# Turning x-hat of a cross-attention block with VectorE blocks and four SBUF transfers instead of TensorE transposes

## What is computed

```python
tgt1 = _layer_norm(tgt, g1, be1)
tgt = tgt + _self_attn(tgt1, mask, Wq, bq, Wk, bk, Wv, bv, Wo, bo)
tgt = tgt + (memory @ Wg.T + bg)
tgt1 = _layer_norm(tgt, g2, be2)
ff = jax.nn.relu(tgt1 @ W1.T + b1) @ W2.T + b2
return tgt + ff
```

## Time and profile before

| | |
|---|---|
| median of 3 runs | 1756.23 us (1755.37 to 1756.37) |
| profiled execution | 1755.81 us, span 1754.0 us |
| PE busy | 1724.6 us, 98% |
| ACT busy | 1432.4 us, 82% |
| DVE busy | 1359.8 us, 78% |
| POOL busy | 802.2 us, 46% |
| DMA | 200.46 MB, mean 114 GB/s |
| granted PE clock | 0.8 to 0.9 of full speed in the first two of 40 slices, then 0.9 or more |

### The profile page before, as it was taken

The page is one execution under the profiler, slowest core; times in us unless marked ns, Lnnn a source line. Parts: engine busy times, 40 slices in busy tenths (PEclk is TensorE's granted clock), DMA queues, the critical chain, the costliest instruction groups (busy, mean ns, idle before and its releaser), DMA issues. The chain is left out here.

```text
span 1754.0 us, 53678 instructions
## 1 busy us (share of the span) xinstructions
PE 1724.6 (98%) x17780; PEld 1698.0 (97%) x17780; DVE 1359.8 (78%) x6945; ACT 1432.4 (82%) x5567; POOL 802.2 (46%) x782
## 2 busy tenths in 40 slices
PE   6799999999999999999999999999999999999998
PEld 6799999999999999999999999999999999999998
DVE  7777777787787777787787877877777877877874
ACT  4788888888888888888888888888888888888883
POOL 4244444444444454444444444444444444444444
PEclk8899999999999999999999999999999999999999
DMA  5333333333333332333433333333333333333320
GB/s 173 106 127 107 115 123 107 120 121 107 122 119 106 124 120 95 132 115 99 135 111 104 129 111 110 128 109 113 124 106 120 121 107 122 118 109 122 119 83 31
DMA packets 185796, 200.46 MB, mean 114 GB/s; under 512 B 18864, under 2 KB 135984, under 8 KB 185520
## 3 DMA queue, kind: packets, MB, share of 16 engines
q1 hardware_dynamic: 185520, 197.02, 33.9%
HBM read 62.73 MB, written 16.78 MB: 45 GB/s over the span
## 5 line engine op out<-in xcount | busy, mean ns | idle before, releaser
L404 ACT ACTIVATE scores<-scores,row_min 128x128 f32<-128x128 f32 x2048 | 795.3, 402 | 11.5 <-DVE row_min L651 11.5
L780 POOL TENSOR_TENSOR hT_lo<-hid,hT_hi 128x512 fp32r<-128x512 f32 x256 | 354.6, 1385 | 516.3 <-DVE hT_hi L685 516.3
L651 DVE CUSTOM_DVE_ANT_0 scores<-score_ps,mask_bias 128x128 f32<-128x128 f32 x2048 | 472.2, 286 | 0.9 <-issue 0.6
L416 ACT ACTIVATE probs<-turn_ps 128x512 f32<-128x512 f32 x512 | 304.8, 596 | 163.7 <-PE turn_ps L916 163.5
L404 ACT ACTIVATION_READ_ACCUMULATOR scores<-scores,row_min 128x1 f32 x2048 | 411.8, 201 | 0.0
L916 PE MATMUL turn_ps<-ident,scores 128*128 128x128 f32 x2048 | 307.6, 273 | 3.1 <-ACT probs L416 3.1
L850 PE MATMUL ffn_ps<-w_hi,hT_lo 128*128 128x256 f32 x1024 | 300.6, 294 | 0.5 <-ACT hid L446 0.5
L850 PE MATMUL ffn_ps<-zT_hi,w_lo 128*128 128x256 f32 x992 | 292.1, 294 | 0.3 <-ACT hid L446 0.3
L852 PE MATMUL ffn_ps<-w_hi,hT_hi 128*128 128x256 f32 x1024 | 284.8, 278 | 0.0
L851 PE MATMUL ffn_ps<-w_lo,hT_hi 128*128 128x256 f32 x1024 | 284.5, 278 | 0.0
L851 PE MATMUL ffn_ps<-zT_lo,w_hi 128*128 128x256 f32 x992 | 276.1, 278 | 0.0
(11 more groups left out here) (136 smaller groups left out, 4268.4 us busy)
## 6 DMA issues: line engine op xcount, KB each, us to landing
q_stack<-q_hi SPq DMA_DIRECT2D x128, 256.0 KB, 2.4
k_stack<-k_hi SPq DMA_DIRECT2D x256, 128.0 KB, 2.3
x_in<-x_dram SPq DMA_DIRECT2D x64, 256.0 KB, 2.6
mem_in<-memory_dram SPq DMA_DIRECT2D x64, 256.0 KB, 3.0
x_res<-x_dram SPq DMA_DIRECT2D x64, 256.0 KB, 3.0
q_stack<-q_lo SPq DMA_DIRECT2D x64, 256.0 KB, 2.4
k_stack<-k_lo SPq DMA_DIRECT2D x128, 128.0 KB, 2.3
inv<-inv_cols SPq DMA_DIRECT2D x256, 64.0 KB, 2.2
```

Source lines behind the costliest of these rows:

```text
L404: last = act.activation(exps, exps, ACT.Exp, bias=row_min[:, k, h:h + 1], scale=-1.0, accum_out=row_sum[:, k, h:h + 1])
L416: act.activation(probs[:, k, :], turn_ps[k % 2][:, :], ACT.Copy).then_inc(probs_copied[k % 2], 1)
L651: last = dve.tensor_tensor_reduce(out=scores[:, slot(i, t), h, :], in0=score_ps[t % 2][:, h * S:(h + 1) * S], in1=mask_bias[:, b, :], scal ...
L780: pool.tensor_tensor(halves[1], src, halves[0], ALU.subtract).then_inc(done, 1)
```

## The change

x-hat of groups 1 to 63 is no longer turned by PE. DVE writes it in place over `x_in`, then turns it in blocks of 32 by 32 with two transposes into `x_quads` (`turn_quads`); four transfers of 64 KB within SBUF carry the blocks back into `x_in` so that each partition holds its feature. POOL makes both parts of `xT` from there, the high part as a product with one; group 1 is split by DVE. Group 0 goes by PE as before. The first norm moves forward in the iteration: statistics at t 3, `rstd` at t 4, apply at t 5, blocks at t 8. The load of x moves to the start of SP's iteration and waits for the split; the store of y moves behind the spread of the inverses. The turn of z stays where it is.

```diff
+        def quad_rows(w):
+            return w[:].rearrange("p b (k c j) -> p b k j c", j=QUADS, c=32)
+        def quad_blocks(w):
+            return w.rearrange("p (j k b r) -> p b k j r", j=QUADS, k=KT, b=GB)
+        def quad_cols(w):
+            return w[:].rearrange("p b n -> p (b n)").rearrange("p (i m r) -> p m i r", i=QUADS, r=32)
+        def in_order(w):
+            return w[:].rearrange("p k (b i r) -> p (k b) i r", b=GB, i=QUADS)
...
             def iteration(i, norm, front, attn_, out_, ffn):
+                if norm and i >= 0:
+                    if i == 0:
+                        sp.wait_ge(x_split, 2)
+                    else:
+                        sp.wait_ge(x_pool_split, i)
+                    sp.dma_start(x_in[:], x_rows[i + 2]).then_inc(x_loaded, 16)
...
+                if norm and i >= -1:
+                    sp.wait_ge(x_blocked, i + 2)
+                    for n in range(QUADS):
+                        sp.dma_start(x_flat[:, n * P:(n + 1) * P],
+                                     x_blocks[32 * n:32 * (n + 1), :].rearrange("c (j n) -> c j n", j=QUADS)
+                                     ).then_inc(x_cols, 16)
...
-                    if front and t == 0 and not high_by_dve(i + 1):
-                        g = i + 1
-                        split_high(by_tile[1], xT[0], x_turned, g + 1, v_ready,
-                                   g if later(g) else None, x_hi)
+                    if is_at(i, -1) and t == 0:
+                        split_high(by_tile[1], xT[0][:], x_turned, 1, v_ready, None, x_hi)
...
+            def turn_quads(g):
+                dve.wait_ge(ln1_ready, g + 1)
+                for b in range(GB):
+                    last = dve.transpose(quad_blocks(x_blocks)[:, b], quad_rows(x_in)[:, b])
+                last.then_inc(x_blocked, 1)
+            def normalise_second():
+                dve.wait_ge(ln1_rstd, 2)
+                dve.tensor_tensor(x_in[:], x_in[:], mv1[:, :, 0:1].broadcast_to([P, GB, D]), ALU.subtract
+                                  ).then_inc(ln1_centred, 1)
+                dve.wait_ge(ln1_centred, 1)
+                dve.tensor_tensor(x_in[:], x_in[:], rstd1[:].unsqueeze(2).broadcast_to([P, GB, D]), ALU.mult
+                                  ).then_inc(ln1_ready, 1)
...
+                    if is_at(i, 0) and t == 0:
+                        dve.wait_ge(x_cols, 16 * QUADS)
+                        dve.wait_ge(v_ready, 1)
+                        dve.tensor_copy(in_order(xT[0]), quad_cols(x_in)).then_inc(early_high, 1)
+                        dve.wait_ge(early_high, 1)
+                        dve.tensor_tensor(in_order(xT[1]), quad_cols(x_in), in_order(xT[0]), ALU.subtract
+                                          ).then_inc(x_split, 1)
...
+                    if norm and i >= 0 and t == 3:
+                        dve.wait_ge(x_loaded, 16 * (i + 3))
+                        layer_norm_stats(i + 2, x_in, stats1, mv1, ln1_rstd, ln1_stats, ln1_mean)
...
+                    if norm and i >= 0 and t == 5:
+                        layer_norm_apply(i + 2, x_in, mv1, rstd1, ln1_rstd, x_in, None, ln1_ready)
+                    if norm and i >= 0 and t == 8:
+                        dve.wait_ge(x_cols, 16 * QUADS * (i + 1))
+                        turn_quads(i + 2)
...
+                    if front and i >= 1 and t == 0:
+                        g = i + 1
+                        pool.wait_ge(x_cols, 16 * QUADS * g)
+                        pool.wait_ge(v_ready, g)
+                        pool.tensor_tensor(in_order(xT[0]), quad_cols(x_in),
+                                           one[:, 0:1].unsqueeze(2).broadcast_to([P, GB * KT, QUADS * 32])
+                                           .rearrange("p m (i r) -> p m i r", i=QUADS), ALU.mult
+                                           ).then_inc(x_pool_hi, 1)
+                        pool.wait_ge(x_pool_hi, g - 1)
+                        pool.tensor_tensor(in_order(xT[1]), quad_cols(x_in), in_order(xT[0]), ALU.subtract
+                                           ).then_inc(x_pool_split, 1)
...
-                    if front and t == 0:
-                        pe.wait_ge(ln1_ready, i + 2)
-                        if not isinstance(i, int) or outs > 0:
-                            pe.wait_ge(z_split, outs)
-                        turn(by_tile[1], xhat).then_inc(x_turned, 1)
```

More of the change, by code:

```diff
@@ L396, in split_high @@
                     act.wait_ge(free, freed)
-                act.activation(dst[:], src, ACT.Copy).then_inc(done, 1)
+                act.activation(dst, src, ACT.Copy).then_inc(done, 1)
             def exponentials(i, k):
@@ L569, in layer_norm_apply @@
                 dve.wait_ge(rstd_done, g + 1)
-                if later(g):
+                if free is not None and later(g):
                     dve.wait_ge(free, g)
@@ L655, in iteration @@
                         last.then_inc(scores_masked, 1)
-                    if front and t == 0:
[L657 to L664, removed]
+                    if is_at(i, -1) and t == 0:
+                        split_low(by_tile[1], xT, x_hi, 1, x_split)
+                    if is_at(i, 0) and t == 0:
[5 more added lines that the diff above has]
+                                          ).then_inc(x_split, 1)
                     if attn_ and t in INVERT_TICKS:
@@ L717, in iteration @@
                         last.then_inc(k_split, 1)
-                    if norm and t == 5:
+                    if norm and i < 0 and t == 5:
                         dve.wait_ge(x_loaded, 16 * (i + 3))
                         layer_norm_stats(i + 2, x_in, stats1, mv1, ln1_rstd, ln1_stats, ln1_mean)
-                    if norm and t == 10:
-                        layer_norm_apply(i + 2, x_in, mv1, rstd1, ln1_rstd, xhat, x_turned, ln1_ready)
+                    if is_at(i, -2) and t == 10:
+                        layer_norm_apply(0, x_in, mv1, rstd1, ln1_rstd, x_first, None, ln1_ready)
+                    if is_at(i, -1) and t == 10:
+                        normalise_second()
+                        dve.wait_ge(x_turned, 1)
+                        turn_quads(1)
+                    if norm and i >= 0 and t == 5:
[3 more added lines that the diff above has]
+                        turn_quads(i + 2)
                     if front and t == 10:
@@ L798, in iteration @@
                         split_low(mem_in[:], [m[:] for m in memT], mem_hi, g + 1, mem_split)
+                    if norm and t == 4:
+                        inverse_root(i + 2, mv1, var1, rstd1, ln1_mean, ln1_var, ln1_ready, ln1_rstd)
                     if out_ and t == 7:
                         inverse_root(i - 1, mv2, var2, rstd2, ln2_mean, ln2_var, ln2_ready, ln2_rstd)
-                    if norm and t == 8:
-                        inverse_root(i + 2, mv1, var1, rstd1, ln1_mean, ln1_var, ln1_ready, ln1_rstd)
                     if out_ and t == 6:
@@ L957, in iteration @@
                         turn_chunk(i - 1, CHUNKS - 1)
-                    if front and t == 0:
-                        pe.wait_ge(ln1_ready, i + 2)
-                        if not isinstance(i, int) or outs > 0:
-                            pe.wait_ge(z_split, outs)
-                        turn(by_tile[1], xhat).then_inc(x_turned, 1)
+                    if is_at(i, -1) and t == 0:
+                        pe.wait_ge(ln1_ready, 1)
+                        turn(by_tile[1], x_first).then_inc(x_turned, 1)
                     if ffn and t in UP_TICKS:
@@ L971, in iteration @@
                         if which == 0:
-                            pe.wait_ge(x_split, i + 2)
+                            if i < 1:
+                                pe.wait_ge(x_split, i + 2)
+                            else:
+                                pe.wait_ge(x_pool_split, i)
+                            if outs > 0:
+                                pe.wait_ge(z_split, outs)
                         elif fronts > 0:
```

26 lines of the change are left out of this document (16 added, 10 removed).

## The result

| | before | changed |
|---|---|---|
| median of the runs | 1755.80 us (1753.77 to 1756.37, 4 runs) | 1735.46 us (1734.68 to 1736.02, 4 runs) |
| profiled execution | 1755.81 us, span 1754.0 | 1734.68 us, span 1732.9 |

The account below looks back on a forecast made before the run. PE's stream was taken as the bound. Sum: -26.4 (PE) + 1.0 (y) + 3.8 (ramp) - 1.6 (next iteration) = -23.2 us, from the median 1733.0 us; range 1727 to 1768.

Parts of the forecast that it names:

- The bound: PE, busy 98% of the span, issues without pause in steady iterations of 26.53 us; a change pays what leaves its stream.
- PE's gain: Four x-hat transposes leave PE's stream in each iteration: 0.44 us, lower bound 0.35; 26.4 us for 60 steady iterations.
- the charge for y: First up-projection waits for y from DVE, 0.04 us of slack: 0.02 us an iteration charged, 1 us in all.
- The apply beside POOL: DVE's two apply instructions stall beside POOL's low part and x_res add, about 0.9 and 1.5 us; DVE 1.2 us later.
- The block turn: Two 128x256 float32 turns on DVE: 0.4 us each, bounds 0.37 and 0.69, z and y keeping their times.
- SP and POOL: Four transfers, 2.57 us to issue, landing 2.2 us after issue; POOL's two passes 2.5 us; 1.0 us slack before q.
- The ramp: Group 1's passes, block turn and transfers delay product q to 38.3 from 34.49: 3.8 us lost, 8.4 if waiting for zeroing.
- the give-back: In the ramp's next iteration, group 2's high and low part and a wait leave DVE: 2.4 less 0.8, 1.6 us back.
- The late split: Rival: POOL's split of x exceeds its 1.0 us slack; 1823 us with passes at twice their price; chance 0.22.
- The block turn doesn't wait for POOL: Judged rival: DVE's block turn waits for POOL's last hidden low part, ending at 818.9; 1753 to 1760 us; chance 0.12.
- The half gain: Rival: x late by 0.1 to 0.2 us, or y by as much; 1739 to 1750 us; chance 0.08.
- sends such a turn to TensorE: Rival: turn belongs on TensorE; block turns up to 0.69 us each take 0.6 us of slack, time stays 1733; no separate chance.

Follow-up runs that it names:

- the first experiment: Changed kernel with four throw-away transposes put back on PE at the x-hat turn's place, groups 2 to 63: 1760.48 us, 26.53 us between chunk turns.
- the up-projection's experiment: Changed kernel with the first up-projection written to the free bank work_ps0, so the second waits for y instead: 1733.73 us, ratio 0.9876.
- the three edits: Changed kernel with group 1 turned by PE, first up-projection in work_ps0, and POOL's x_res add ahead of rstd, together: 1727.71 us, ratio 0.9847.
- the three with the late add: Changed kernel with group 1 on PE, up-projection in work_ps0, and POOL's early x_res add only from iteration 4 on: 1726.52 us, ratio 0.9838.

## Why the prediction was right

- *The bound.* PE, and only steps of its stream: right, and the first experiment turned it off and on.
- *PE's gain, 0.44 us less 0.02 for y, an iteration.* 0.41 measured, 24.65 us for sixty instead of 25.4, but in part by luck. The two steps were 0.44 and 0.35. Which one is left depends on whether the product behind waits: without a wait it is 0.35 (the up-projection in a free bank), with y it is 0.45. So the gross gain was 0.44 and the charge for y was mis-sized, 0.09 instead of 0.02: at its place the change saved 0.79 - 0.45 = 0.34 us, and 0.36 up to the q product (4.46 behind the chunk turn before, 4.10 now). The last 0.05 came from where the forecast had no term: the k products, from the first to the chunk turn behind them, took 1.51 us (829.56 to 831.07) and now take 1.46 (821.96 to 823.42), in the medians too. They take 1.50 again with PE's transposes back (the first experiment) and 1.51 with passes added on POOL, so it goes together with how late PE comes there; why is not shown. These 3 us of the total hid the most part of the missed wait for y. The trace of before had the remaining step once, in its last iteration, where there is no x to turn, and I didn't look there (y ended at 1697.30, 0.14 us ahead of the product):

```profile
1696.99 0.60 PE L916 MATMUL turn_ps<-ident,scores 128*128 128x128 f32 x4
1697.44 0.35 PE L850 MATMUL ffn_ps<-zT_hi,w_lo 128*128 128x256 f32 x1
```

- *The apply beside POOL.* 2.4 us for the two (0.9 and 1.5) were forecast, and 2.39 measured, against 0.88 unhindered. The second ended 0.29 us behind POOL's add, the very distance that the ramp had shown. The Trainium skill's "SBUF — State Buffer", Who interferes with whom, was weighed there, and the trace agrees: 966 ns with the add beside it, 478 without.
- *The block turn.* 0.4 us each taken, 0.62 measured, inside the range of 0.37 to 0.69. Statistics of the same size were the wrong neighbour for a strided read; with a contiguous one it is 0.42.
- *SP and POOL.* 2.58 us to issue, 2.1 us to land, 1.04 and 1.29 us for the passes: as the rows said, with no surcharge for runs of 32 elements. The slack was put at 1.0 and was 1.03 in the median. The turns ended 3.5 us ahead of the chunk turn (810.63 to 814.15), where 3.7 was forecast; POOL's shorter low part (1.29 for 1.35) and the q product, 4.10 behind the chunk turn instead of 4.02, gave that back.
- *The ramp.* Group 1's loss of 3.4 us was forecast as 3.8, with its steps in place: the second pass ended at 31.24, the high part didn't wait for the zeroing. *The step that failed is the give-back*: 1.6 us forecast, 0.45 seen at group 2's q product and gone again at 69.25. I counted what leaves DVE in that iteration, but PE hadn't waited for it: before, `xT_lo` of group 2 was ready at 57.85, and the q product started at 59.77 behind PE's own work. What came back was the turn of x-hat in PE's stream. And the statistics of x, which cost nothing in the steady part, stand ahead of `q_lo` at their new place and made PE wait 1.03 us more for it, in the experiment with group 1 on PE too. So the ramp cost 3.85 instead of 2.2; 4.2 by the experiment with group 1 on PE.
- *The rivals.* The late split occurs once in the change's profile, 0.74 us in the ramp, and not in the steady part. Its price is confirmed by the period, 1.34 us more for 1.26 of lateness. That two extra passes gave 1827, where the sum said 1823, is partly luck: they add 2.24 us and not 2.5, and 5.4 us of it lie in the ramp (first steady chunk turn at 114.20). The block turn doesn't wait for POOL (590 to 648 ns in all 126). The half gain would have been the wait for y, which is 0.09 and not 0.2. The Trainium skill's "VectorE: DVE Perf Modes", The three transpose paths and Rules for kernel authors, sends such a turn to TensorE; here TensorE is the bound, and the change, 0.41 us an iteration faster without it there, is on the other side.

## What to carry to other kernels

Where one engine's stream sets the period, price a removed instruction by the step between starts, and look for an iteration of the old trace in which it is already missing: that shows what stands behind it. A turn by VectorE and transfers has a long latency (7.8 us here from the block turn's start to the split's end), so it fits where a stage's lead is longer than that, and not in this ramp, where each stage waited for the one before: leave the first groups as they were. Work moved into an engine's idle time is free only in the iterations that have that idle time. Before making a hidden chain's engine or the bound faster, read the least slack of all iterations, not of a typical one.

## What the runs showed of the hardware that I had not expected

*A block transpose's length depends on the stride of its read.* 128x256 in float32: 0.42 us contiguous, 0.62 reading every fourth element. It has one input from SBUF and ran beside POOL's subtraction without a stall, where the apply stalled.

*One issue of a transfer in some is longer, on a fixed beat of instructions.* SP takes 2.57 us for these four nearly always, but

```profile
1124.08 3.39 SPq L390 DMA_DIRECT2D x_in<-x_quads  x4
...
1254.69 3.48 SPq L390 DMA_DIRECT2D x_in<-x_quads  x4
```

and so in every fifth iteration (2.75 to 3.48), which is where the slack of the split falls, to 0.13 us at the least in the steady part, and where the waits of the up-projection's experiment lie. With two extra passes on POOL the long ones were at

```profile
495.75 2.88 SPq L390 DMA_DIRECT2D x_in<-x_quads  x4
...
633.42 2.74 SPq L390 DMA_DIRECT2D x_in<-x_quads  x4
```

again five iterations apart, though these took 27.5 us each, so it goes with the count of iterations and not by time. Other issues have the same in the iterations between (the store of y took 1.66 us at 816.71, against 0.37 at least). What does it, no run here shows.

*The clock in the ramp differs between executions, of one program too.* The windows view (PE, PEld, DVE, ACT and POOL busy, granted clock, DMA share, GB/s) of the three edits, and then of the three with the late add:

```profile
20.00:30.00 10.00, 7.70 (x45) 7.32 (x44) 9.60 (x14) 6.56 (x6) 7.89 (x5) 0.61 0.43 154
```

```profile
20.00:30.00 10.00, 5.70 (x35) 5.42 (x34) 9.74 (x12) 5.54 (x4) 8.58 (x5) 0.83 0.43 153
```

In the second the k products of group 0 were 0.12 us apart from 16.4 us on, in the first 0.21, the steps of 2.4 and of 1.2 GHz for the same 256 columns, after the same work. (The granted clock reads 1.00 from 16 to 20 us in both; there only the steps tell them apart.) It was 0.66 against 0.50 from 30 to 40 us and 0.83 against 0.76 from 40 to 60. The second was 1.47 us ahead at 45.37 (46.84 in the first) and 2.18 at 78.78 (80.96). It is the profiled execution, and the fastest, of its five. One and the same program differs so too: in the change's two profiled executions the step fell at 18.1 and at 16.6 us, and the clock granted from 20 to 30 us was 0.66 and 0.83; they ended within 0.2 us all the same. A lead in the clock is thus not always kept, and that the clock made all of the 2.18 us is not shown. The five executions of the last version span 3.1 us, so 2 us between single ones are not to be put down to an edit.
